# Expert blocks: router weights' transposes and second-bias products moved behind the last block, one table load moved ahead of the zero fills, and a new order of steps

## The reference, cut to what matters

```
out[token] = sum over the two chosen experts e of
                 w[token, e] * ( act(x[token] @ W1[e] + b1[e]) @ W2[e] + b2[e] )
```

## Time and profile before

| what | us |
|---|---|
| median of 3 runs | 2206.45 (2192.79 to 2210.58) |
| the profiled execution, its own time | 2201.29 |
| its span, first to last instruction | 2199.5 |
| PE busy in the span | 1780.3 (81%) |
| DVE busy | 1419.9 (65%) |
| ACT busy | 1029.4 (47%) |
| mean granted clock of TensorE | 0.923 of full |

### The profile page before, as it was taken

One profiled execution on the slowest core, in us unless ns is written; L12 is line 12 of the kernel. 1 busy time (PEld: TensorE's weight loads), 2 busy tenths in 40 slices (PEclk: granted clock), 3 DMA queues, 4 the chain that ended last, 5 costly groups with the idle time before them and its releaser, 6 DMA issues.

```text
span 2199.5 us, 40006 instructions
## 1 busy us (share of the span) xinstructions
PE 1780.3 (81%) x14664; PEld 1383.0 (63%) x14664; DVE 1419.9 (65%) x4926; ACT 1029.4 (47%) x2564; POOL 387.5 (18%) x354
## 2 busy tenths in 40 slices
PE   6588996989998577677999788889985957776786
PEld 5455684767666355455898576666655955564675
DVE  5588522877776477687767666667766356657843
ACT  2277423666665456566222245444442525552342
POOL 3300100000001000000100300000155445213443
PEclk9899998999999689999999889999997978887898
DMA  4233192000001878777100323222203652423366
GB/s 170 68 98 101 59 327 71 1 1 2 1 1 36 225 200 225 214 218 201 77 1 1 81 68 100 68 70 70 68 21 111 201 170 66 107 52 116 96 205 195
DMA packets 210603, 228.96 MB, mean 104 GB/s; under 512 B 15508, under 2 KB 178732, under 8 KB 209768
## 3 DMA queue, kind: packets, MB, share of 16 engines
q1 hardware_dynamic: 205416, 216.10, 34.6%
q0 software_dynamic: 4992, 10.30, 1.4%
HBM read 130.96 MB, written 94.98 MB: 103 GB/s over the span
## 4 chain that ended last, share of the span: by engine, by line
PE 43%; DVE 21%; DMA 18%; SPq 6%; ACT 5%; issue 4%; POOL 3%; DVEq 0%; ACTq 0%; POOLq 0%
PE banks L689 37%; SPq L2562 6%; DMA skew<-region 4%; DMA stacks<-region 4%; ACT P L1433 3%; PE banks L1004 2%; DMA skew_room<-sorted 2%; DVE region L1820 2%; DVE P L1753 2%; POOL sorted L2443 2%; DVE negm L1764 2%; DMA back<-mask,block_to 1%; DVE region L1753 1%; DMA kz<-stacks 1%; ACT region L1433 1%
## 5 line engine op out<-in xcount | busy, mean ns | idle before, releaser
L2403 POOL TENSOR_TENSOR norms<-norms,consts 128x2 f32<-128x2 f32 x112 | 80.7, 721 | 1445.3 <-DVE norms L1757 1444.7
L1433 ACT ACTIVATE P<-P,negm 128x256 f32<-128x256 f32 x512 | 240.9, 498 | 148.8 <-DVE negm L1990 87.9
L1433 ACT ACTIVATE P<-banks 128x512 f32<-128x512 f32 (+2 forms) x392 | 185.7, 511 | 162.3 <-PE banks L689 158.8
L689 PE MATMUL banks<-xnT,region 128*128 128x256 f32 x672 | 182.9, 387 | 10.3 <-ACT xnT L1433 7.0
L1764 DVE TENSOR_REDUCE negm<-banks 128x2 f32<-128x512 f32 (+1 forms) x264 | 147.6, 589 | 42.2 <-PE banks L689 39.5
L689 PE MATMUL banks<-kz,qs 128*128 128x256 bf16 (+1 forms) x512 | 124.7, 278 | 56.5 <-DVE negm L1990 27.1
L689 PE MATMUL banks<-region 128*32 128x256 f32 (+6 forms) x922 | 128.5, 366 | 39.3 <-ACT region L1433 17.3
L689 PE MATMUL banks<-bands,identb 128*128 128x160 bf16 (+1 forms) x768 | 141.6, 249 | 0.0
L689 PEld LDWEIGHTS banks<-xnT,region 128*128 128x128 f32 x672 | 122.2, 192 | 30.4 <-ACT xnT L1433 10.5
L689 PE MATMUL banks<-qs,kz 128*128 128x256 bf16 (+2 forms) x512 | 116.7, 270 | 29.5 <-DMA kz<-stacks 16.1
L689 PE MATMUL banks<-kz,region 128*128 128x256 f32 x512 | 132.4, 380 | 0.3 <-ACT kz L1433 0.3
(11 more groups left out here) (288 smaller groups left out, 4459.1 us busy)
## 6 DMA issues: line engine op xcount, KB each, us to landing
stacks<-region SPq DMA_DIRECT2D x178, 192.0 KB, 3.0
sorted<-qs SPq DMA_DIRECT2D x4, 4160.0 KB
skew<-region SPq DMA_DIRECT2D x64, 256.0 KB
qs<-stacks SPq DMA_DIRECT2D x24, 408.0 KB
kz<-stacks SPq DMA_DIRECT2D x48, 192.0 KB
skew<-region SPq DMA_DIRECT2D x64, 128.0 KB
skew_room<-skew SPq DMA_DIRECT2D x32, 256.0 KB
P<-skew SPq DMA_DIRECT2D x32, 256.0 KB
```

The source lines that it names most:

```text
L689: return p.e.matmul(o, lhsT, rhs, start=start, stop=stop)
L1433: return a.e.activation(o, i, f, **kw)
L2403: g.e.tensor_tensor(room[:, :, 0], room[:, :, 0], pows[:, :], ALU.pow).then_inc(done, 1)
```

## The change

* `route_ahead` loses its last two steps on PE, its last on ACT and its last on DVE: the transpose of `w`, the copy to `wT`, the product with b2 and its addition to x.
* `sorted_experts` gets them behind its last block, for all four items of the stream at once: two groups of four transposes (banks T and S0), two ACT copies of 8x512, two groups of four products (banks S1 and V), and four DVE additions in two steps. The products have 8 rows of contraction (`b2[0:E, :]`) where they had 128.
* `w` is kept for four items. `wT` is no tile of its own any more, it lies in the room of the blocks' rows. Two memsets of the old `wT` on POOL go.
* Block 0 on PE waits for `placed` (the four items' rows placed) where it waited for `x_part`. The combination on DVE waits for the additions of its pair of items.
* SP issues the `rel` DMA in front of the zero fills, and in front of the wait for `behind_zero`.
* All five orders in `TURNS` are new.

```
@@ route_ahead on PE
-                p.wait_ge(s.routed, p.next(s.routed))
-                p.clear(s, "route")
-                for t in range(TOK):
-                    i = p.e.transpose(s.T[0:E, t * 128:(t + 1) * 128], s.w[:, t, :], ident)
-                i.then_inc(s.f_full, 1)
...
-                for t in range(TOK):
-                    i = mm(s.T[:, t * D:(t + 1) * D], s.wT[:, t * 128:(t + 1) * 128], b2)
@@ sorted_experts on PE
-                p.wait_ge(s.x_part, 3 * ITEMS + ITEMS * (w + 1))
+                p.wait_ge(s.placed, (ITEMS + 2) * w + ITEMS)
...
                 yield from down(BLOCKS - 1)
+                for a, (name, bank) in enumerate((("T", s.T), ("S0", s.S0))):
+                    yield
+                    p.wait_ge(s.routed, ITEMS * (w + 2))
+                    p.clear(s, name)
+                    for n in range(2 * TOK):
+                        i = p.e.transpose(bank[0:E, n * 128:(n + 1) * 128], s.w[:, TOK * a + n // TOK, n % TOK, :], ident)
+                    i.then_inc(s.to_scalar, 1)
+                    p.fill(s, name, s.hidden)
+                    hidden[BLOCKS + a] = p.free[s.n, name]
+                for a, (name, bank) in enumerate((("S1", s.S1), ("V", s.V))):
+                    yield
+                    p.wait_ge(*hidden[BLOCKS + a])
+                    p.wait_ge(load_sem["b2"], 16)
+                    p.clear(s, name)
+                    for n in range(2 * TOK):
+                        i = mm(bank[:, n * D:(n + 1) * D], s.wT[:, a, n * 128:(n + 1) * 128], b2[0:E, :])
+                    i.then_inc(s.to_vector, 1)
+                    p.fill(s, name, s.x_part)
@@ sorted_experts on ACT
+                for k, bank in enumerate((s.T, s.S0)):
+                    yield
+                    a.wait_ge(s.to_scalar, a.next(s.to_scalar))
+                    act(s.wT[:, k, :], bank[0:E, :]).then_inc(s.hidden, 1)
@@ sorted_experts on DVE
+                    for a, bank in enumerate((s.S1, s.V)):
+                        yield
+                        v.wait_ge(s.to_vector, v.next(s.to_vector))
+                        for n in range(2):
+                            x_n = xb(own_batches[s.n][2 * a + n])
+                            i = tt(x_n, x_n, bank[:, n * TOK * D:(n + 1) * TOK * D].rearrange("p (t d) -> p t d", t=TOK), ALU.add)
+                        i.then_inc(s.x_part, 1)
...
-                v.wait_ge(s.x_part, 3 * ITEMS + ITEMS * w + k + 1)
+                v.wait_ge(s.x_part, 3 * ITEMS + 2 * w + k // 2 + 1)
@@ L0_ffn on SP
                 for z in streams:
                     d.wait_ge(z.x_done, j)
+                dma(rel, bass.AP(tensor=rel_vec_d.tensor, offset=0, ap=[[1, 128], [2 * S, H], [1, S + 128]]), rel_back_sem)
                 for z in streams:
                     d.wait_ge(z.behind_zero, 1)
...
-                dma(rel, bass.AP(tensor=rel_vec_d.tensor, offset=0, ap=[[1, 128], [2 * S, H], [1, S + 128]]), rel_back_sem)
```

More of the change, by code:

```diff
@@ L52 @@
 TURNS = {
[L53 to L82, removed]
@@ L389, in __init__ @@
         self.small = sb("small", [4, TOK])
-        self.w = sb("w", [TOK, E])
+        self.w = sb("w", [B // 2, TOK, E])
         self.picks = sb("picks", [2, TOK, E * R], BF16)
@@ L394, in __init__ @@
         self.pick_w = sb("pick_w", [2, TOK])
-        self.wT = sb("wT", [S])
         self.counted = sb("counted", [B, E], BF16)
@@ L408, in __init__ @@
         self.block_x = self.block_rows[:, :, 0:D]
+        self.wT = skew_space[0:E, 0:B // 2 * S].rearrange("e (a c) -> e a c", a=2)
         self.block_to = sb("block_to", [6], I32)
@@ L646, in full_before @@
     def full_before(j):
-        return before(j, 3, 5)
+        return before(j, 3, 3)
     def out_before(j):
-        return before(j, 2, 2)
+        return before(j, 2, 1)
     def lane_base(w, k):
@@ L1257, in run, with sorted_experts @@
                 p.fill(s, "route", s.logits_out)
[L1258 to L1272 removed]
             return run
[L1275 removed]
+        def sorted_experts(w, pack, w1, w2, b2):
             def run(s, b, j):
@@ L2152, in run @@
                 step(v.e.reciprocal(den, den))
-                tt(s.w[:, :, :], ew, wide(den), ALU.mult).then_inc(s.routed, 1)
+                tt(s.w[:, item, :, :], ew, wide(den), ALU.mult).then_inc(s.routed, 1)
                 yield
                 v.wait_ge(s.routed, v.next(s.routed))
-                step(tt(each, both, s.w[:, :, :].unsqueeze(1).to_broadcast([128, 2, TOK, E]), ALU.mult))
+                step(tt(each, both, s.w[:, item, :, :].unsqueeze(1).to_broadcast([128, 2, TOK, E]), ALU.mult))
                 step(red(pw, each, ALU.add))
-                yield
-                v.wait_ge(s.f_full, start + 5)
-                tt(xb(b), xb(b), s.T[:, 0:TOK * D].rearrange("p (t d) -> p t d", t=TOK), ALU.add).then_inc(s.x_part, 1)
-                v.next(s.x_part)
             return run
@@ L2538, in gpsimd_program @@
         g.e.memset(b2rows[:, :], 0.0)
-        for s in streams:
-            g.e.memset(s.wT[:, :], 0.0)
         g.e.memset(ones_b[:, :], 1.0).then_inc(consts_sem, 1)
```

150 lines of the change are left out of this document (84 added, 66 removed).

## The result

The median after is 2139.12 us (four runs, 2135.82 to 2141.53), against 2204.39 for the kernel before beside it: a ratio of 0.9709, 95% interval 0.9665 to 0.9752. The forecast was 2171, range 2138 to 2212. The direction is right and the time lies at the lower edge of the range; 65 us went where 35 were forecast. The profiled execution took 2135.82 us.

What follows compares the result with a forecast made beforehand. PE was the busiest engine at 81% of the span, so its idle time could be won. 2201.3 - 16.9 - 4 + 1 - 16 = 2165.4 us profiled, a median near 2171 us, range 2138 to 2212.

Steps and rivals of the forecast that it cites:

- The forecast's own last part: Signs in the profile after; failure if layer 1's cross-attention changes over 15 us or idle time reappears in layer 3's attentions.
- The `rel` load, 16.9 us: Before layer 1's self-attention: load issued ahead of the zero fills, PE's wait of 15.0 us goes whole, 16.9 us together.
- The routing steps, 4 us: Steps taken from 16 routing items: fewer stops of PE and DVE, 4 us won, bounds nothing to 38.6 us.
- their new place, -1: Same steps behind the last block of each expert layer: 1 us lost, bounds nothing or 2 us at each end.
- estimate of the cover: At the kernel's end: moved steps take about 5.5 us, just under DVE's 5.9 us idle before the combination.
- The order, 16 us: New order of both streams' steps: (a), (b) and (c) together win 16 us, bounds 0 and 45.
- (a): Before the first expert layer: resident-weight blocks fill idle PE time, 5 us of 23.6.
- (b): Behind the first expert layer: both streams go into layer 3 together, 8 of 33 us idle PE time won.
- (c): Last layer: stream 1's blocks begin 34 steps sooner, 3 of 33 us idle PE time won.
- Layer 1's cross-attention, 0 us: Stage of 330 us, taken as bound by its transfers; no gain in the sum, a small loss expected at most.
- Rival 2: Layer 1's cross-attention: streams in step lose 16 us at each of three more common starts, 48 us, median 2235; chance 0.12.
- Rival 3: Layer 1's cross-attention: transfers in step fill DMA engines better, a third of 54 us won, 2153 us; chance 0.14.

Runs made afterwards that it cites:

- first experiment: The kernel before with one edit, the load of `rel` issued ahead of the zero fills, in the old order: 2187.92 us, ratio 0.9915.
- last experiment but one: The kernel before with only the order changed, up to a point in layer 1's self-attention, load behind the fills: 2210.46 us against 2218.48, ratio 0.9962.

## Why the prediction was right and wrong

The time lies in the range by 1 us, and the gain of 65 us is nearly twice the forecast's 35. That the sum came so near is in part luck: two terms of it are worth nothing or less in the changed kernel, and the stage that gave the most stood in it with nothing. The forecast's own last part says that it fails if layer 1's cross-attention changes by more than 15 us, and that stage became 35 us shorter.

**The bound.** Right: PE's idle time was what could be won. PE's busy time hardly changed, its share rose from 81 to 83%.

**The `rel` load, 16.9 us.** 15.0 of it is the wait. The other 1.9 is the difference between two times of four matmuls of 512 columns: 3.78 us right behind the wait, where the mean granted clock was 0.51 (344.4 to 348.3 us), and 1.88 at 355.05, where it was 1.00 (355 to 357). The same pair gives the factor of two in the bounds of the moved steps. In the wait itself the granted clock was 0.50 (340 to 344 us); that the idle time lowered it was the author's estimate, no run shows what sets it. The size was right for the load alone in the old order (16.4, first experiment), the 1.9 with it: the matmuls that read `rel` begin there at 330.80 with no wait, and four of them take 1.88 us at a granted clock of 1.00 (330.8 to 332.7). Whose gain it is was wrong. In the changed kernel the load's new place is worth nothing (2139.23 us without it against 2139.12), because the new order covers the wait by itself. It does so at a price of 5 to 8 us (8 won where 16.4 was to be had, last experiment but one), which its order of the self-attention makes up. The sentence "The item of stream 1 that is queued behind the wait on PE moves up with it, and in the new order stands ahead of it" held the answer, and the forecast drew no conclusion from it. Self-attention therefore starts at 347 us and not at 330, and its first addition comes 10 us sooner than before (401.8 to 391.6), not 15 to 17.

**The routing steps, 4 us, and their new place, -1.** In the old order the two together cost about 7 us by the medians, some 3 by the traces, where a gain of 3 was forecast. The stops of PE and DVE were worth nothing that a run shows, the bottom of the bounds. The estimate of the cover was good: some 5.5 us of steps in the 5.9 us of the transfer, and from the last copy to the combination it is 6.2 us, as before, even where PE's granted clock was 0.50. The 0.2 us for a hop between engines was an estimate; in the trace of before PE starts at 2185.11, 0.15 us behind the end of the copy of DVE that it waited for (2184.96). What the estimate left out is the order, where both streams end together and there is less of a gap: there the steps cost 2 us, the upper bound for one end.

**The order, 16 us.** Measured 56 on the changed code, above the bound of 45. Three sub-terms. (a) and (b), 5 and 8: together the order behind layer 2's cross-attention gave 33 in the total; the stretch from there to the combination got 42 shorter, and a part was given back on both sides of it: layer 2's attentions became 14 us longer, and layer 3's, as the prediction's last part said they might, 10. The mechanism, resident blocks filling idle time and streams that end together, was right. Its share of the idle time was not: 13 of 57 us were taken, and the two windows of the same stretch show 25 of 47 gone. Nor did it count the clock there, whose mean went from 0.83 to 0.92. (c), 3: from layer 3's last attention addition to the end of the last combination it is 115 to 116 us in the four traces with the new order and 118 to 123 in the six with the old, all on the changed code, so some 5. It is as much without the moved steps (112.4 against 116 to 120), so their new place has no part in it.

**Layer 1's cross-attention, 0 us.** This is the step that failed most: the stage was left out of the forecast, as rivals 2 and 3 stood against each other. Rival 2 read a loss from the common start (PE 18.1 us of work in 40). But that start is the same in both orders, as it holds the change of blocks (from 691 to 731 us PE works 13.0 us in either), and the later borders repeat it only in small: with the new order up to layer 2 PE works 29 to 31 us in the 40 around each, and 34 to 36 in the 40 between them. Rival 3 was right in sign, and in mechanism for the part that hangs on bytes. There it was nearly right in size too, by luck, as nothing in the rows spoke for a third: a third of 54 is 18, the runs give 17. The other 13 us were not in it; 30 in the stage, 21 to 25 after what the feed-forward gives back. That the stage "is bound by its transfers" was too much said: with a quarter of the bytes gone, the old order's stage became 6% shorter. What spoke for rival 3 in the rows was the share of 79% beside 95% in the fullest part, and a wait of SP that the prediction didn't read: 85.8 us on its own transfers' landing, by the list of waits of the kernel before.

So the sum by steps: forecast 17 for the load, 3 for the moved steps and 16 for the order; measured, one upon the other, 16, -7 and 56. Undone last, the load costs nothing, so its 16 could as well be booked to the order. What no run separates is how much of the 13 us of the cross-attention that don't hang on bytes are SP's queue and how much the chain across PE, DVE and ACT; and the value of the moved steps under the new order, beyond the 2 us at the end, wasn't tried.

## What to carry to other kernels

Price the parts of a change in the order in which they will run: a wait that one part removes may be one that another part already covers, and then only one of the two counts. When two streams share engines and one queue of transfers, look at how far apart they run in every long stage and how each stage ends: a stream that ends alone leaves idle time that its own chain can't fill (at the end of the changed code with the old order PE stopped for 2.8, 1.2 and 2.6 us in 10, and its granted clock was then 0.50). A stage in which no engine is over 72% busy and the DMA engines are at 75% can still yield 30 us of 351 to a better interleaving, so an unsaturated stage is not a reason to price an order change at nothing.

## What was not expected of the hardware

- With the DMA engines at a mean share of only 75% (207 GB/s), halving the bytes of the skewed transfers of three items in four, and nothing else, made it 21 us shorter (351 to 330); in the better order, with a share of 80%, only 5 us (321 to 316). A mean share well under full doesn't say that bytes are free.
- The same eight transposes and eight products (16 records) took 1.04 and 2.05 us at a granted clock of 1.00, or 1.91 and 3.78 at one of 0.50; the latter behind three stops of 1.2 to 2.8 us. Yet from the last copy to the combination it was 6.2 us, as in the kernel before, where that time goes to a transfer: what waits longest by name need not cost anything.
- The kernel before had a median of 2204 us on some chips and 2218 on another, more than several of the effects measured here. Only ratios to runs beside it can be compared.
